# Self attention of layer 1: the inverse of the softmax sums made on ScalarE as exp(-ln(sum)) in place of a reciprocal on VectorE

## The reference, cut to what matters

```
q, k, v = split(einsum('bsd,ed->bse', layernorm(x), Wqkv))        # 16 heads of 8
logits  = einsum('bihd,bjhd->bhij', q, k) * 8**-0.5 + pos_bias
attn    = softmax(logits)
out     = einsum('bsd,ed->bse', einsum('bhij,bjhd->bihd', attn, v), Wout)
x       = x + out
```

## Time and profile before

| | us |
|---|---|
| median of 3 runs | 1470.76 |
| lowest, highest | 1470.67, 1476.12 |
| span of the profiled execution | 1470.8 |
| s4 in it | 714 to 956 |

### The profile page before, as it was taken

How to read it: one execution, slowest core, us unless ns; L and a number is a source line. 1 busy time by engine, 2 the same in 40 slices (tenths; PEclk the granted TensorE clock), 3 DMA queues, 4 the chain that set the end, 5 groups by cost and what they waited for, 6 DMA issues and landing times.

```text
span 1470.8 us, 38209 instructions
## 1 busy us (share of the span) xinstructions
PE 1379.5 (94%) x14581; PEld 1051.8 (72%) x14581; DVE 917.2 (62%) x2370; ACT 796.8 (54%) x1526; POOL 655.2 (45%) x680
## 2 busy tenths in 40 slices
PE   6999999997999989999789998899999999998997
PEld 5667667666777777887556666678888888885864
DVE  3344444436889975435789988785677767766123
ACT  4544545444788864545467675655545455542521
POOL 3344445334326642006777776543334444443034
PEclk9999999999999999999899999999999999999999
DMA  5020330000475812237000000000000000001323
GB/s 164 20 66 23 89 118 8 12 1 6 178 281 210 288 51 82 80 122 276 23 10 2 2 2 2 2 14 6 7 2 11 12 12 8 9 11 50 111 59 90
DMA packets 97820, 92.60 MB, mean 63 GB/s; under 512 B 21869, under 2 KB 71658, under 8 KB 97386
## 3 DMA queue, kind: packets, MB, share of 16 engines
q1 hardware_dynamic: 93034, 80.71, 16.9%
q0 software_dynamic: 4608, 9.45, 2.1%
HBM read 31.92 MB, written 58.21 MB: 61 GB/s over the span
## 4 chain that ended last, share of the span: by engine, by line
PE 77%; DVE 9%; ACT 6%; issue 4%; POOL 3%; DMA 1%; SPq 1%; DVEq 0%; ACTq 0%; POOLq 0%
PE bank L3238 6%; PE bank L1641 5%; PE bank L1625 5%; PE bank L3273 5%; PE bank L3252 4%; PE bank L3226 4%; PE bank L947 4%; PE bank L874 4%; PE bank L880 4%; PE bank L903 3%; PE bank L924 3%; PE bank L2611 3%; PE bank L2621 3%; PE bank L3264 2%; PE bank L891 2%
## 5 line engine op out<-in xcount | busy, mean ns | idle before, releaser
L1407 ACT COPY s_pT<-bank 77x512 f32<-77x512 f32 (+1 forms) x256 | 134.7, 584 | 70.0 <-PE bank L1625 69.9
L3010 POOL TENSOR_TENSOR s_p<-s_p,s_inverse 128x616 f32<-128x616 f32 x64 | 76.9, 1221 | 202.1 <-DVE s_inverse L3153 202.1
L1625 PE MATMUL bank<-ident,s_p 128*77 128x128 f32 (+1 forms) x1024 | 140.4, 284 | 18.9 <-ACT s_p L1398 18.5
L1625 PEld LDWEIGHTS bank<-ident,s_p 128*77 128x77 f32 (+1 forms) x1024 | 116.3, 148 | 46.8 <-ACT s_p L1398 30.5
L1294 POOL TENSOR_TENSOR s_p<-s_p,s_peak 128x1024 f32<-128x1024 f32 x64 | 120.1, 1897 | 39.8 <-DVE s_peak L1493 39.8
L1398 ACT ACTIVATE s_p<-s_p 128x616 f32<-128x616 f32 (+1 forms) x128 | 110.7, 888 | 26.2 <-POOL s_p L1294 22.5
L3137 DVE TENSOR_REDUCE s_peak<-bank 128x8 f32<-128x616 f32 x64 | 50.8, 793 | 93.7 <-PE bank L3252 93.7
L753 DVE TENSOR_TENSOR s_aT<-bank,s_weight 128x512 f32<-128x512 f32 (+1 forms) x64 | 44.1, 690 | 96.9 <-PE bank L924 58.1
L3238 PE MATMUL bank<-pos_bias,s_ctx 128*32 128x128 f32 x3072 | 90.5, 274 | 1.7 <-ACT s_kT L3048 1.7
L3068 ACT ACTIVATE s_p<-s_p 128x616 f32<-128x616 f32 x64 | 46.8, 731 | 81.8 <-DVE s_p L3141 81.8
L1479 DVE TENSOR_TENSOR s_p<-bank,pos_bias 128x1024 f32<-128x1024 f32 x64 | 77.6, 1216 | 18.2 <-PE bank L1614 18.2
(11 more groups left out here) (366 smaller groups left out, 3380.9 us busy)
## 6 DMA issues: line engine op xcount, KB each, us to landing
sorted_tokens<-s_zero SPq DMA_DIRECT2D x4, 5632.0 KB
sorted_tokens<-s_zero SPq DMA_DIRECT2D x8, 2560.0 KB, 13.2
routed_tokens<-s_routed SPq DMA_DIRECT2D x24, 256.0 KB, 2.3
s_tokens<-sorted_tokens SPq DMA_DIRECT2D x48, 64.0 KB, 1.9
s_rows<-sorted_tokens SPq DMA_DIRECT2D x48, 64.0 KB, 1.9
x_all<-x SPq DMA_DIRECT2D x8, 256.0 KB, 3.0
w_s_gateup<-s_gateup SPq DMA_DIRECT2D x1, 2048.0 KB
out<-x_all SPq DMA_DIRECT2D x8, 256.0 KB, 2.9
```

The source lines that it names most:

```text
L1407: nc.scalar.copy(pT[0:keys, b % 2, 4 * q:4 * q + 4, :].rearrange("m h t -> m (h t)"), bank[0:keys, flip_bank("p", b, q), :]).then_inc(drai ...
L1625: last = nc.tensor.transpose(bank[0:keys, into, j * T:(j + 1) * T], p[:, b % 2, 4 * q + j, :], core.ident[:, :])
L3010: nc.gpsimd.tensor_tensor(part, part, inverse[:, b % 2, heads].unsqueeze(2).to_broadcast([P, HU, M]), ALU.mult).then_inc(share_ready, 1)
```

## The change

VectorE's reciprocal of the sums is taken out of this stage (it stays in the cross attention). ScalarE makes the inverse with two instructions: Ln from PSUM into `inverse`, a wait on itself, and Exp with scale -1 in place. The pair stands in step s for batch s-2, after `exp_of`, the first half of `keep_pT` and whatever `keep_k`, `keep_q` or `keep_v` the step has, and ahead of the second half of `keep_pT`; for the last batch it stands in a step of its own. It waits for `weighed` (TensorE's sums) and `o_ready` of the batch before (VectorE has read the tile). VectorE's product waits for the pair. The activation table loaded at the stage's start is the set that has both Ln and Exp.

```diff
+    log_ready = sem(s + "_log_ready")
...
+        def inverse_of(b):
+            act.wait_ge(weighed, b + 1)
+            if b:
+                act.wait_ge(o_ready, b)
+            nc.scalar.activation(inverse[:, :], bank[:, WORK, B:B + T], ACT.Ln).then_inc(log_ready, 1)
+            act.wait_ge(log_ready, b + 1)
+            nc.scalar.activation(inverse[:, :], inverse[:, :], ACT.Exp, scale=-1.0).then_inc(inverse_ready, 1)
+
...
-        nc.scalar.preload_act_table_set("exp_and_others")
+        nc.scalar.preload_act_table_set("exp_and_others" if cross else "natural_log_exp_and_others")
         before.memory(act)
-        for step in range(BATCH + 1):
+        for step in range(BATCH + 1 if cross else BATCH + 2):
             b, g = step - 1, step // G + 1
+            if step > BATCH:
+                inverse_of(step - 2)
+                continue
...
             if step % G == 1 and step < BATCH:
                 keep_v(step // G)
+            if not cross and step >= 2:
+                inverse_of(step - 2)
             if b >= 0:
                 keep_pT(b, 1)
...
         def head_outputs(b):
             dve.wait_ge(weighed, b + 1)
-            nc.vector.reciprocal(inverse[:, :], bank[:, WORK, B:B + T]).then_inc(inverse_ready, 1)
+            if cross:
+                nc.vector.reciprocal(inverse[:, :], bank[:, WORK, B:B + T]).then_inc(inverse_ready, 1)
             dve.wait_ge(inverse_ready, b + 1)
```

## The result

| | before | after |
|---|---|---|
| median, us | 1471.48 | 1479.75 |
| lowest, highest | 1470.67, 1476.12 | 1476.86, 1482.24 |
| runs | 5 | 5 |
| span of the profiled execution | 1470.8 | 1479.0 |
| its PE, DVE, ACT busy | 1379.5, 917.2, 796.8 | 1380.2, 889.0, 812.9 |

After / before is estimated at 1.0049, with a 95% interval of 1.0033 to 1.0066: slower by about 7 us (the medians lie 8.3 apart), where +5.9 was the forecast. VectorE has 28 us less to do, ScalarE 16 us more, and the program takes longer.

The account below looks back on a forecast made before the run. TensorE was taken to set the pace, 25.16 us busy plus 2.20 us of pauses per 27.36 us period. 3.2 + 3.0 - 0.3 = +5.9 us on 1470.76 gave 1476.6 us, range 1472 to 1482.

Parts of the forecast that it names:

- VectorE was the bound after all: Rival: VectorE's list sets the pace, so removing the reciprocal saves 16 us, giving 1454 us; chance 0.03.
- The pair's duration: On ScalarE: Ln 0.29 us, Exp 0.31, 0.03 between them, 0.10 overlap; what stands behind moves by 0.53 us.
- Kind 1: Steps 5, 9 to 25, pair behind the copy of v: TensorE's pause grows from 1.01 to 1.54 us; +3.2 us.
- Kind 2 and kind 0: Steps with step % 4 of 2 or 0: the pair fits ScalarE's idle gap before the pT copies; cost 0.
- Kind 3: Steps 7, 11, 15, 19, pair behind the copy of q: product 1.04 us late, next bias 0.74; +3.0 us.
- Step 23: Sums of results behind the product are held until GpSimd is done, so a 1.04 us later start costs nothing.
- The end of the stage: Last batches run one after another: twice -0.31 us, some 0.3 back from step 28's late copies; together -0.3 us.
- The rival of the clock: Longer TensorE pauses halve its clock, some 2.6 us each, one to three times: 1479.2 to 1484.4 us; chance 0.20.
- The base: Starting time for the sum: the median of the runs, 1470.76 us, taken as the profiled span of 1470.8 within 0.1.
- Pair dearer: Rival: ScalarE's overlaps around the pair are lost, +8.6 us, so 1479.4 us; chance 0.12.
- Delay absorbed: Rival: VectorE's missing 0.95 us helps elsewhere, or the pair is cheaper; +0 to +3, 1471 to 1474 us; chance 0.14.
- Table loads: Rival: Ln and Exp in different sets bring 64 loads onto ScalarE, 82 us at most, 1553 us; chance 0.01.

Follow-up runs that it names:

- A free inverse: Kernel before the change with the reciprocal made for the first batch only, its result used for all 32, nothing added to ScalarE; one run, 1467.99 us.
- both early kernels: Changed kernel with the pair moved ahead of the copy of q alone, 1473.51 us in its first run, or of the copy of v alone, 1472.32 us.
- the last of the experiments with the normalisations: Changed kernel, pair left late, with two normalisations moved ahead of the copy of v; one run, 1472.96 us.
- the pair early everywhere: Changed kernel with the pair moved up behind the first half of keep_pT in every step; median 1473.28 us, ratio to before 1.0006.
- the early normalisations: Kernel before the change with two normalisations moved ahead of the copy of v; median 1470.69 us against 1472.35, ratio 0.9987.

## Why the prediction was right, and where not

The forecast was slower by 5.9 us; the span is slower by 8.2 and the medians by 8.3, and 1479.75 lies inside the range of 1472 to 1482. The sign and the two places were right, and their sizes within 12%. The time came out 3 us above the 1476.6, by the clock and by the base, neither of which is in the sum; it lies above the 1474.5 to 1478 given to the forecast by itself, in the part of the range that was kept for the slower rivals. Step by step:

- **What bounds the kernel.** Right. A free inverse leaves the period at 27.36, so VectorE's 24.97 us of work was no bound, and the rival "VectorE was the bound after all" is out.
- **The pair's duration.** Ln 0.278, Exp 0.310, 0.03 between them; 0.29 and 0.31 were taken. The second pair of rows, one function over 288 and over 512 columns, gave the Exp to 0.01 us. The stretch of the list grew by 0.50 instead of 0.53 us.
- **Kind 1.** Right in mechanism and size: 6 x 0.505 = 3.0, forecast 3.2. Moving the pair in this step alone gives it back.
- **Kind 2 and kind 0.** Right at 0: in both early kernels the two other terms leave nothing over, and the pair of kind 2 is taken up in the gap that was read. ScalarE's timeline in step 10, which answers to the earlier trace rows:

```profile
797.74 0.28 ACT L1415 ACTIVATE s_inverse<-bank 128x128 f32<-128x128 f32 x1 [0.43 <-PE bank L1656]
...
798.36 1.07 ACT L1408 COPY s_pT<-bank 128x512 f32<-128x512 f32 x2
```

The copies start 3.66 us after TensorE's transposes at 794.70, and 3.65 after those at 792.74 before.
- **Kind 3.** Right in mechanism, 12% too large: 4 x 0.65 = 2.6, forecast 3.0. The product is 1.07 us late (forecast 1.04). Less the idle 0.30 that is 0.77, but the bias is only 0.68 late, since it now follows on the moments without a wait and starts a little ahead of their end; and the bias is 0.03 shorter. The forecast used the rule that neighbours overlap on ScalarE and forgot it on VectorE.
- **Step 23.** The held sums behave as read: L2168 starts 1.1 us later against GpSimd's subtraction and is only 3.18 us long, where it took 4.04. L2168 is L2153 of before. The step costs 0.21, not 0. The timeline of step 23, GpSimd and VectorE:

```profile
891.75 3.75 POOL L1295 TENSOR_TENSOR s_p<-s_p,s_peak 128x1024 f32<-128x1024 f32 x2
...
894.43 3.18 DVE L2168 SCALAR_TENSOR_TENSOR x_all<-s_tokens,s_share,x_all 128x128 f32<-128x128 f32 x8
```

The sums end at 897.61, 2.1 us after GpSimd's end at 895.50 (1.85 before).
- **The end of the stage.** Right in sum, and in part by luck: two errors nearly cancel. With the clock full it is read from the last of the experiments with the normalisations, which has the late pair too: 20.56 us from the addition of batch 27 to that of batch 31, instead of 20.78. That is -0.22, where -0.3 was forecast. Of its parts the gain is -0.73 and not twice -0.31, as the pair early everywhere shows, and the late pair gives 0.51 back and not 0.3. In the profile of the change a fall of the clock hides this: it goes through the weighing of batch 30, whose two halves last 1.94 and 1.76 us instead of 1.08 each. TensorE's timeline there:

```profile
954.60 1.94 PE L1656 MATMUL bank<-s_pT,s_v 128*32 128x128 f32 x32
...
956.31 1.76 PE L1656 MATMUL bank<-s_pT,s_ones 128*32 128x128 f32 x32
```

- **The rival of the clock.** The forecast left it out and gave it 0.20; it came in addition. Of the 2.3 us between 5.9 and 8.2 it makes 1.9: 1.61 in the steady part and 1.6 at the end, less the 1.3 of the stretch after step 23, which had cost more before. The second profile of the change has the same three. It was priced at 2.6 us a fall and costs 1.61, since the half clock ends within the weighing: the eight transposes last 1.81 instead of 1.09 and the 64 matmuls 2.85 instead of 1.96, not the 3.64 of the earlier trace rows. As a choice of "does it happen or not" the rival was put wrongly. Seven falls in six profiles say that it belongs in the forecast as a term of its own, with hindsight 7/6 x 1.61 = +1.9. One argument against it, that TensorE is busy on both sides of the new pause, did not hold.
- **The base.** The forecast added to the median, 1470.76, because the profiled span was 1470.8. But every run that shows both lies 1.8 to 1.9 us above its span, so an execution with a span of 1470.8 is one of 1472.6. The wider medians of before are 1471.5 to 1472.4, about 1 us up. The two should have been kept apart.
- **The other rivals.** *Pair dearer* (overlaps lost): no, the pair's neighbours overlap as forecast. *Delay absorbed*: hardly. The front gains 0.21 us, once, up to the first addition, which the sum had at nothing, and no later batch of it gains. *Table loads*: no. The page "ScalarE: Activation LUTs" of the Trainium skill (Table sets) says that one set has both Ln and Exp and one load is enough for them. The trace agrees: Ln takes at most 283 ns and Exp at most 314 in all 32 batches, and the stage's line of the table load has two loads in the whole span, one for each stage that the function serves, as before.

## What to carry to other kernels

Work moved to an engine with spare time is paid for by its place in that engine's list: ask what the instruction ahead of it waits for, and who stands behind the one that waits for its result. Here both prices were nothing one or two instructions earlier, where the engine stood idle anyway, and the same gap had room for the normalisations too. Before such a change, run the kernel with the operation left out: here it would have told that less than 3 us were to be had at most, and nothing in the steady part.

## What the runs showed of the hardware

- TensorE's clock fell to 1.2 GHz behind 7 of 36 single pauses of 1.51 to 1.54 us between busy stretches, at a different place in each execution, and behind none of 48 pauses of 1.01 us and less in the same steps. Two of 14 pauses of 1.34 us were followed by a fall, and all 14 of 3.00 to 4.19. Half a microsecond more of pause carried 1.61 us of slow matmuls with it wherever the clock fell.
- Two executions of one kernel with the same period differed by 8.3 us in span, and five falls of the clock made 8.0 of them.
- An inverse of 128x128 sums in PSUM takes VectorE 948 ns as a reciprocal, and ScalarE 278 + 30 + 310 ns as Ln and Exp.
- A shorter period did not arrive whole: six pauses shorter by 0.76 us made 3.8 us in the stage and 1.7 in the median, since a step that waits for another engine (step 23) gave 0.64 back.
- Eight additions of VectorE over three SBUF operands last 2.31 us alone, and 3.18, 4.04 or 4.68 the more of them runs beside GpSimd's subtraction (and the profiles of the change and of the early normalisations).
